# Weights staged through one f32 buffer, and one prepass buffer less, in a four-layer kernel on 8 cores

## The reference

```
L0 attn  xk,xv,xr = x*tm + shift(x)*(1-tm);  k = xk Wk.T; v = xv Wv.T; r = sigmoid(xr Wr.T)
         a = ew*a + e^k*v;  b = ew*b + e^k;  out = r * (eu*e^k*v + a)/(eu*e^k + b);  out Wo.T
L0 ffn   h = silu(x w1.T s1) * (x w2.T s2);  h = gelu(h h1.T);  h = gelu(h h2.T);  h w3.T s3
L1 attn  bitlinear(x, n, w): xn = rmsnorm(x)*n;  xn is rounded to 8 bits by its row's maximum;
         w is rounded to -1, 0, 1 times mean|w|.  q,k,v,g,gk from bitlinear;  o = gated scan;
         bitlinear(o*silu(g), no, wo)
L1 ffn   bit_linear(x, w1), depthwise conv of 3 taps, silu, bit_linear(., w2)
```

## Time and profile before

| | |
|---|---|
| median of 3 runs | 11883.48 us (11873.69 to 11897.56) |
| profiled execution | 11940.95 us |
| its span, slowest core (core 2) | 11939.4 us |
| spans of the 8 cores | 11831.5 to 11939.4 us |
| busy share of the span | TensorE 46%, VectorE 28%, ScalarE 15%, GpSimd 3% |

### The profile page before, as it was taken

The page is one execution under the profiler, slowest core; times in us unless marked ns, Lnnn a source line. Parts: engine busy times, 40 slices in busy tenths (PEclk is TensorE's granted clock), DMA queues, the critical chain, the costliest instruction groups (busy, mean ns, idle before and its releaser), DMA issues.

```text
span 11939.4 us, 72147 instructions; the slowest of 8 cores (11831.5 to 11939.4 us)
## 1 busy us (share of the span) xinstructions
PE 5443.8 (46%) x22678; PEld 2600.3 (22%) x22678; DVE 3383.9 (28%) x5916; ACT 1836.4 (15%) x2558; POOL 387.3 (3%) x777
## 2 busy tenths in 40 slices
PE   3430016666666666666653343433433343334333
PEld 1120002222222222222222222222222222112112
DVE  6762231000000100000014434434434433453453
ACT  1222101000000000000013112122112223121121
POOL 0000110000000000000000000000000000000000
PEclk8765558888888788877776666666666666656656
DMA  4223432222222222222211111111201101011012
GB/s 116 76 76 116 141 105 39 41 44 45 43 43 43 39 42 43 42 42 38 41 32 57 45 44 61 60 37 54 74 31 60 60 21 34 26 31 57 26 31 80
DMA packets 169144, 637.24 MB, mean 53 GB/s; under 512 B 24832, under 2 KB 25216, under 8 KB 157504
## 3 DMA queue, kind: packets, MB, share of 16 engines
q0 software_dynamic: 81088, 237.61, 10.6%
q1 hardware_dynamic: 87680, 395.02, 9.7%
HBM read 794.50 MB, written 42.01 MB: 70 GB/s over the span
## 4 chain that ended last, share of the span: by engine, by line
PE 42%; DVE 24%; DMA 19%; issue 7%; ACT 6%; DVEq 1%; POOL 1%; ACTq 0%; SPq 0%; POOLq 0%
PE ps L825 17%; PE ps L777 5%; DMA f_wj<-h1R 4%; DMA f_wj<-h2R 4%; PE ps L1742 2%; PE ps L1102 2%; PE ps L862 2%; PE ps L1640 2%; DMA f_wj<-w1R 2%; PE ps L1269 2%; PE ps L1399 2%; DMA pre_in<-f1T 1%; DMA pre_in<-f2T 1%; PE ps L1083 1%; DMA b_wj<-q_f2T 1%
## 5 line engine op out<-in xcount | busy, mean ns | idle before, releaser
L825 PE MATMUL ps<-f_h,f_wj 128*128 128x512 bf16 x8192 | 2078.9, 421 | 1114.0 <-DMA f_wj<-h1R 557.7
L825 PEld LDWEIGHTS ps<-f_h,f_wj 128*128 128x128 bf16 x8192 | 868.5, 106 | 2324.4 <-issue 1652.2
L873 DVE SCALAR_TENSOR_TENSOR XA<-ps,SVEC,XA 128x512 f32<-128x512 f32 x32 | 24.0, 751 | 3556.7 <-PE ps L862 3554.4
L777 PE MATMUL ps<-f_h,f_wj 128*128 128x512 bf16 x2048 | 573.7, 450 | 525.9 <-DMA f_wj<-w1R 519.0
L836 ACT ACTIVATE f_h<-ps,f_sc 128x512 bf16<-128x512 f32 x256 | 175.9, 687 | 2966.5 <-PE ps L825 2954.3
L1742 PE MATMUL ps<-b_hc,b_wj 128*128 128x512 bf16 x1024 | 293.2, 457 | 481.5 <-DVE b_hc L1474 360.5
L777 PEld LDWEIGHTS ps<-f_h,f_wj 128*128 128x128 bf16 x2048 | 229.4, 112 | 869.8 <-issue 714.5
L1102 PE MATMUL ps<-a_wl,a_xqf 128*128 128x512 bf16 x1024 | 294.3, 457 | 139.8 <-DMA a_wl<-q_gwT 61.5
L797 DVE SCALAR_TENSOR_TENSOR f_h<-ps,f_sc,f_g 128x512 bf16<-128x512 f32 x128 | 96.1, 751 | 782.0 <-ACT f_g L787 775.3
L862 PE MATMUL ps<-f_h,f_wj 128*128 128x512 bf16 x1024 | 252.4, 412 | 138.8 <-DMA f_wj<-w3R 138.8
L1249 PE MATMUL ps<-a_qg,a_kp 128*128 128x128 f32 x256 | 76.4, 454 | 523.6 <-DVE a_kg L1242 523.6
(11 more groups left out here) (345 smaller groups left out, 7349.6 us busy)
## 6 DMA issues: line engine op xcount, KB each, us to landing
f_wj<-h1R POOLq DMA_DIRECT2D x128, 512.0 KB, 6.6
f_wj<-h2R POOLq DMA_DIRECT2D x128, 512.0 KB, 6.4
a_wl<-q_owT SPq DMA_DIRECT2D x32, 2048.0 KB, 7.3
b_wj<-q_f2T SPq DMA_DIRECT2D x80, 512.0 KB, 4.4
pre_in<-f1T SPq DMA_DIRECT2D x64, 512.0 KB, 4.2
pre_in<-f2T SPq DMA_DIRECT2D x64, 512.0 KB, 3.9
a_wl<-q_vwT SPq DMA_DIRECT2D x16, 2048.0 KB, 7.2
a_wl<-q_gwT SPq DMA_DIRECT2D x16, 2048.0 KB, 7.2
```

The source lines that it names most:

```text
L777: t.matmul(PS[bank][:, :], wb[:, i, :], XB[:, i, s2 * 512:(s2 + 1) * 512], start=(i == 0), stop=(i == NC - 1)),
L825: off=off, SRC=SRC: t.matmul(PS[bank][:, :], wb[:, i2, :], SRC[:, i * 1024 + off:i * 1024 + off + 512], start=(i == 0), stop=(i == 31)),
```

## The change

Four things. The L0 weights are loaded in f32 into one staging buffer of 128x1024 and cast by VectorE into the bf16 tiles: each DMA waits for the cast before it, and the casts stand in VectorE's queue ahead of all else of the stage. The prepass has two input buffers instead of three. NB and NGK2 are f32 tiles, loaded without a cast. NOB is loaded in f32 into a part of V that isn't in use yet, and VectorE casts it, between the first two operations of its queue in layer 1 attention.

```diff
@@ -292,7 +292,7 @@
 
         pre_stack = ExitStack()
         pre = dict(
-            ins=[sb(f"pre_in{i}", [128, 1024], F32, pre_stack) for i in range(3)],
+            ins=[sb(f"pre_in{i}", [128, 1024], F32, pre_stack) for i in range(2)],
             outs=[sb(f"pre_out{i}", [128, 1024], BF16, pre_stack) for i in range(2)],
             acc=sb("pre_acc", [128, 1], F32, pre_stack),
             reds=[sb(f"pre_red{i}", [128, 1], F32, pre_stack) for i in range(2)],
@@ -371,7 +371,7 @@
     state = {"g": None, "v": None, "s": None, "tread": None,
              "ld": [None, None, None], "qd": [None, None, None],
              "redf": [None, None]}
-    NR = 3
+    NR = 2
     for nm, di, do in QW:
         wi = QWI[nm]
         src, dst = din[nm], qscr[nm]
@@ -484,13 +484,19 @@
         CARA = sb("l0_carA", [128, NC, 1], F32, st_)
         CARB = sb("l0_carB", [128, NC, 1], F32, st_)
 
+        WSTG = [sb(f"l0_wstg{i}", [128, 1024], F32, st_) for i in range(1)]
         wtok = None
-        first = True
+        wst_free = [None]
+        wi0 = 0
         for Wb, nm in ((WK, "wkT"), (WV, "wvT"), (WR, "wrT"), (WO, "woT")):
             for c in range(NC):
-                wtok = P.dma("g", Wb[:, c, :], din[nm][c * 128:(c + 1) * 128, :],
-                             new=first)
-                first = False
+                sl0 = 0
+                d = P.dma("g", WSTG[sl0][:], din[nm][c * 128:(c + 1) * 128, :],
+                          after=[wst_free[sl0]], new=True)
+                wtok = P.op("v", lambda v, Wb=Wb, c=c, sl0=sl0: v.tensor_copy(
+                    Wb[:, c, :], WSTG[sl0][:]), after=[d, wtok])
+                wst_free[sl0] = wtok
+                wi0 += 1
 
         v0 = P.op("v", lambda v: v.memset(CARA[:], 0.0))
         v0 = P.op("v", lambda v: v.memset(CARB[:], 0.0), after=[v0])
@@ -919,9 +925,9 @@
         A2 = sb("a_a2", [128, 128], F32, st_)
         OG = sb("a_og", [128, 2048], BF16, st_)
         OQF = sb("a_oqf", [128, 16, 128], BF16, st_)
-        NB = sb("a_nb", [128, 1024], BF16, st_)
+        NB = sb("a_nb", [128, 1024], F32, st_)
         NOB = sb("a_nob", [128, 2048], BF16, st_)
-        NGK2 = sb("a_ngk2", [128, 16], BF16, st_)
+        NGK2 = sb("a_ngk2", [128, 16], F32, st_)
         G1T = sb("a_g1t", [128, 2, 16], F32, st_)
         X2Q = sb("a_x2q", [16, 256], BF16, st_)
         WGK1 = sb("a_wgk1", [128, 8, 16], BF16, st_)
@@ -931,13 +937,16 @@
 
         P.barrier()
         d_ngk2 = P.dma("g", NGK2[:], din["ngk2B"], new=True)
-        d_nob = P.dma("g", NOB[:], din["noB"], new=True)
+        d_nob = P.dma("g", V[:, 0, :], din["noB"], new=True)
         d_wgk1 = P.dma("y", WGK1[:, :, :],
                        qscr["gk1wT"].rearrange("(c p) n -> p c n", p=128), new=True)
         d_wgk2 = P.dma("y", WGK2[:, :], qscr["gk2wT"], new=True)
 
         vz = P.op("v", lambda v: v.memset(S[:], 0.0))
-        vz2 = P.op("v", lambda v: v.memset(STAT[:, 62:63], 0.0), after=[vz])
+        nob_tok = P.op("v", lambda v: v.tensor_copy(NOB[:], V[:, 0, :]),
+                       after=[vz, d_nob])
+        d_nob = nob_tok
+        vz2 = P.op("v", lambda v: v.memset(STAT[:, 62:63], 0.0), after=[nob_tok])
         vt = vz2
         gt = None
         nb_free2 = [None, None]
```

## The result

The changed kernel takes 12103.13 us (median of 8 runs, 12069.31 to 12135.33), the kernel before 11882.09 beside it (8 runs). The ratio is 1.0181, 95% interval 1.0159 to 1.0204: 0.0181 × 11882 = **215 us slower**. The prediction said 12074, from +191; its range was 12015 to 12150.

What follows compares the result with a forecast made beforehand. No engine was taken to bound the whole kernel; stages wait on different things. The terms 118 + 51 + 17 + 5 = 191 us, added to the median of 11883.48, gave 12074 us (+1.6%), range 12015 to 12150.

Steps and rivals of the forecast that it cites:

- Part 1: Start of layer 0: L0 weights through one f32 buffer delay the first mix operation from 60.85 to 179 us, +118 us.
- the turn: Staged L0 weights: DMA, VectorE cast and hand-overs to the next DMA take 5.1 us a tile once xT is in.
- the 37 us to the first matmul: Start of layer 0: TensorE's first matmul comes 37 us after the first mix operation.
- the 41 us for xT: Start of layer 0: xT is in at 41 us, with five staged weight tiles of about 7.5 us by then.
- staged loads land slowly: Rival, 9%: staged L0 weight loads take 5.2 us each, the mix starts at 216 us, +155, total 12111 us.
- the start is absorbed: Rival, 3%: the delay at the start is given back because the prepass tail has its own pace; total 11956 us.
- Part 2: Prepass first pass: two input buffers give 2.83 us a tile, +0.64 us on each of 80 exposed tiles, +51 us.
- Part 3: Layer 1 attention: NB in f32 makes each L992 multiply 0.53 us longer, 32 of them on the path, +17 us.
- no term depends on the clock: Whole kernel: the same 191 us is added to either the profiled execution or the median.
- Part 4: Start of layer 1 attention: VectorE waits for the noB load and casts it, +4.7 us, once.
- Sum: Whole kernel: 118 + 51 + 17 + 5 = 191 us, 12074 us when added to the median; this forecast had 78%.
- TensorE's clock rises in the L0 FFN: Rival, 2%: a higher mean clock there makes the kernel faster; +0.02 would give 11834 us.

Runs made afterwards that it cites:

- the run of this part alone: Kernel before with only the L0 weights loaded through one f32 buffer and cast by VectorE: 11998.23 us, ratio 1.0105.
- alone +52: Kernel before with only the prepass input buffers cut from three to two: ratio 1.0135 (0.9822 to 1.0448), prepass tail +52.4 us.
- the four-buffer run: Kernel before with four prepass input buffers instead of three: 11843.8 us beside 11915.25, one run.
- The run without f32: Kernel before, NB still bf16, with one more VectorE bf16 copy behind each multiply of L992: layer 1 attention 3445.8 us, +31.4.
- the prefetching kernel: Kernel before, with second-pass prepass loads waiting only for their buffer, no longer for VectorE's last operation on the previous tile: 11577.57 us, ratio 0.9722.

## Why the prediction was right, and where its sizes were off

**Part 1 (+118; measured +126).** The mechanism, the turn (5.1; 5.05) and the 37 us to the first matmul held, and so did the 41 us for xT: it has landed at 38 to 41 us, some 20 us sooner than before. The eight missing us lie in the first five turns. I had them over at 41 us, and the fifth was cast at 48.5 as a mean of the cores (51.89 on the slowest). I took 7.5 us a turn beside xT, and it was 10 to 12: after a first load of 5.7 us, the three beside xT landed in 9 to 11. The fifth, issued behind xT's landing, met two loads of the prepass and took 8.3 us on the slowest core, 3.7 to 5.9 on the others. The Trainium skill's fit (DMA: Bandwidth & Descriptors, Anatomy of one DMA) gave 3.2 us a load and an estimated turn of 4.7 us; the trace has a median landing of 3.5 and a turn of 5.05, and does not agree. The rival "staged loads land slowly" needed a turn of 6.7 and fell; "the start is absorbed" fell with the run of this part alone (+127.4 at the start, and nothing given back behind it).

**Part 2 (+51; +50, alone +52).** Right in mechanism, and the size came out closer than its parts. The landing was 4.2 against 4.3, but a tile of f1T took 2.98 us on average against 2.83. The added time a tile was 0.79 us for f1T, 0.68 for owT and 0.59 for f2T, where the prediction took f1T's 0.64 for all. Over the 80 tiles that makes 55 us, of which the tail shows 50. Owing to the four-buffer run, that latency and buffers bound the pass is shown and not only argued. As predicted, the second pass did not change (7.16 before, 7.17 after, f1T on core 2).

**Part 3 (+17; +31).** The term that was mis-sized. Its first half held: 1226 ns a multiply, forecast 1227, and VectorE no longer idle. From a multiply to the end of the rounding a projection takes 0.65 us longer and not 0.53: 32 × 0.65 = 21 us. The matmul chains add 13 us. Together that is 34, beside the 31 measured; the rest lies beside other work. The 13 I had excluded by saying that no term depends on the clock: this is the step that failed, and the chains of k show it, at a mean clock of 0.72 instead of 0.83. The run without f32 shows that another delay of this size at this place does the same.

**Part 4 (+4.7; +4.3 at the stage's start).** noB landed after 10.6 us and the cast took 1.23. Whether the 4.3 reach the end of the stage these runs can't tell.

**Sum.** 191 against 210 by stages and 215 by the timing. Of the 19 missing by stages 8 are Part 1's and 12 layer 1 attention's (33.6 against 17 + 4.7), less 1 of Part 2. The rival that TensorE's clock rises in the L0 FFN did not occur: in the stretch of the earlier trace rows, 176 us later, the changed kernel has the same 0.84. Where the clock did move, in layer 1 attention, it made the kernel slower.

## What to carry to other kernels

A ring of DMA, engine and next DMA costs its whole turn per tile; divide the time that a buffer takes to come round (landing, hand-over, work) by the number of buffers, and expect that time to grow with each further load in flight, here by 6 to 11% (means of the cores: 5.1 to 5.4 in the ring, 6.0 to 6.6 to 7.3 in the first pass). How many buffers it takes until bandwidth binds was not tried. Before pricing buffers, look for loads that wait for more than their own buffer: dropping one such wait was worth 2.8%, more than anything the buffers did. And where TensorE works in bursts, as in this layer 1 attention, a delay ahead of a burst can cost more than itself (here 31 us for 21 of delay); a dummy operation of the same length measures it.

## What the runs showed that I had not expected

With a pause longer by 0.63 us ahead of two short transpositions, the next chain of 64 matmuls took 1.06 us longer in the block shown, at a mean clock of 0.72 instead of 0.83 in it; over all blocks and cores 0.8 us longer.

A GpSimd load of 512 KB lands in 3.5 us (median) by itself, and in 9 to 11 us beside SyncE's load of xT.

In the prefetching kernel, GpSimd's issue of a store and VectorE's operations lengthen each other. First one issue of the kernel before, with VectorE idle beside it, then the second pass over f1T with prefetch:

```profile
1234.11 0.89 POOL L81 DMA_DIRECT2D q_f1T<-pre_out  x1 [3.52 <-DVE pre_out L439]
```

```profile
1154.74 0.75 DVE L433 TENSOR_SCALAR pre_in<-pre_in,pre_rs 128x1024 f32<-128x1024 f32 x1
1155.60 0.69 DVE L436 TENSOR_SCALAR pre_cmp<-pre_in 128x1024 f32<-128x1024 f32 x1
1155.67 1.11 POOL L81 DMA_DIRECT2D q_f1T<-pre_out  x1 [3.64 <-DVE pre_in L433]
...
1158.31 0.89 POOL L81 DMA_DIRECT2D q_f1T<-pre_out  x1 [1.53 <-DVE pre_out L439]
1158.66 1.02 DVE L436 TENSOR_SCALAR pre_cmp<-pre_in 128x1024 f32<-128x1024 f32 x1
...
1161.35 1.23 DVE L439 SCALAR_TENSOR_TENSOR pre_out<-pre_in,pre_cmp 128x1024 bf16<-128x1024 f32 x1 [1.67 <-DMA q_f1T<-pre_out]
```

Who begins first is not held up. L436 takes 0.69 us ahead of the issue at 1155.67, and 1.02 behind the one at 1158.31. That issue takes 0.89 us, as a store of f1T does with nothing beside it (the 0.54 of the earlier trace rows is a store of owT); the one at 1155.67, which begins while L436 runs, takes 1.11. The Trainium skill (SBUF — State Buffer, SBUF: two separate sides) says that GpSimd and a VectorE operation in a two-port mode share a pair of ports, and that whichever starts first has it for its whole instruction. These rows agree in kind, with 0.2 to 0.3 us each; waiting for the other's end would have cost L436 0.54 us and the issue 0.62, so they don't show a wait for the whole instruction. The last row shows the next bound: VectorE now waits for a store to free one of the two output buffers.
